# A fourth of the one-hot tiles made by ScalarE, in the preparation stage of a graph-network kernel on Trainium2

## What is computed

```python
w_full = einsum('rb,bdo->rdo', w_comp, weight)      # R=16 types from B=8 bases
x_rel  = einsum('nd,rdo->rno', feat, w_full)        # feat: layer-normed x
msg    = x_rel[etypes, src] * norm
agg    = segment_sum(msg, dst, num_segments=N)
out    = relu(agg + h_bias + feat @ loop_weight)
```

## Time and profile before

| | |
|---|---|
| median of 3 runs | 2738.4 us (2736.8 to 2740.6) |
| profiled execution | 2740.9 us, span 2738.9 us |
| mean granted TensorE clock | 0.919 |
| PE busy | 2204.7 us (80%) |
| POOL busy | 1789.0 us (65%) |
| DVE busy | 952.1 us (35%) |
| ACT busy | 651.5 us (24%) |
| `expand`, first spread to last coefficient copy | about 81.5 to 147.0 us |

### The profile page before, as it was taken

How to read it: one execution, slowest core, us unless ns; L and a number is a source line. 1 busy time by engine, 2 the same in 40 slices (tenths; PEclk the granted TensorE clock), 3 DMA queues, 4 the chain that set the end, 5 groups by cost and what they waited for, 6 DMA issues and landing times. The chain is left out here.

```text
span 2738.9 us, 41332 instructions
## 1 busy us (share of the span) xinstructions
PE 2204.7 (80%) x11549; PEld 1840.7 (67%) x11550; DVE 952.1 (35%) x2094; ACT 651.5 (24%) x1539; POOL 1789.0 (65%) x1888
## 2 busy tenths in 40 slices
PE   2789999999999888887676767557666589999988
PEld 0667787877777666666565555446444479999976
DVE  7734233242243222221321212112112733333339
ACT  3523323233223211211111010000000323222246
POOL 0657777777777777777777777777775045555545
PEclk9999999999999999998898888788777799999999
DMA  7544444444444444444343443333333631222237
GB/s 246 155 138 124 132 116 121 125 124 145 117 124 120 134 120 120 121 121 131 109 121 116 121 116 106 109 105 116 107 105 80 250 138 69 69 70 69 69 110 257
DMA packets 146287, 338.71 MB, mean 124 GB/s; under 512 B 36719, under 2 KB 56335, under 8 KB 145981
## 3 DMA queue, kind: packets, MB, share of 16 engines
q0 software_dynamic: 89328, 245.33, 30.6%
q1 hardware_dynamic: 39351, 59.54, 6.3%
q10 hardware_dynamic: 17526, 32.88, 3.7%
HBM read 292.84 MB, written 47.97 MB: 124 GB/s over the span
## 5 line engine op out<-in xcount | busy, mean ns | idle before, releaser
L1063 POOL DMA_INDIRECT rows<-feat,srcT x1540 | 1460.7, 948 | 491.2 <-issue 439.6
L1266 PE MATMUL psW<-rows,S 128*128 x3920 | 1049.4, 429 | 357.4 <-SPq L1034 325.4
L1266 PEld LDWEIGHTS psW<-rows,S 128*128 128x128 f32 x3920 | 830.7, 216 | 572.1 <-issue 439.5
L1137 DVE TENSOR_TENSOR S<-psHere,coefS 128x896 f32<-128x896 f32 x280 | 301.9, 1090 | 1307.4 <-PE psW L1266 1294.9
L1326 ACT COPY z<-psW 128x512 f32<-128x512 f32 x196 | 114.7, 585 | 1389.3 <-PE psW L1266 1388.7
L1232 PE MATMUL psG<-wb,zT 128*128 128x256 f32 (+1 forms) x1600 | 356.0, 381 | 0.0
L1232 PEld LDWEIGHTS psG<-wb,zT 128*128 128x128 f32 (+1 forms) x1600 | 298.6, 188 | 45.2 <-ACT zT L1337 0.2
L1716 PE MATMUL psH<-xT,w1x 128*128 128x128 f32 x1840 | 227.2, 277 | 2.7 <-issue 2.7
L1667 POOL DMA_INDIRECT expert_rows<-os,at_rows x114 | 116.8, 1024 | 170.7 <-DVE os L1775 170.7
L1716 PEld LDWEIGHTS psH<-xT,w1x 128*128 128x128 f32 x1840 | 216.9, 194 | 4.4 <-issue 4.4
L1725 PE MATMUL psO<-w2s,hT 128*128 x912 | 215.7, 379 | 0.0
(11 more groups left out here) (279 smaller groups left out, 1405.0 us busy)
## 6 DMA issues: line engine op xcount, KB each, us to landing
rows<-feat,srcT POOLq DMA_INDIRECT x1568, 2.7
g<-expert_rows SPq DMA_DIRECT2D x24, 512.0 KB, 5.6
w1s<-in_L_ffn_w SPq DMA_DIRECT2D x8, 1024.0 KB, 9.8
w2s<-in_L_ffn_w SPq DMA_DIRECT2D x16, 512.0 KB, 9.9
feat<-rows SPq DMA_DIRECT2D x24, 256.0 KB, 3.0
fts<-feat ACTq DMA_DIRECT2D x24, 256.0 KB, 2.9
h<-in_x ACTq DMA_DIRECT2D x24, 256.0 KB
y_rows<-y ACTq DMA_DIRECT2D x24, 256.0 KB
```

Source lines behind the costliest of these rows:

```text
L1063: e.indirect_dma_start(rows[:, j % RB * H:(j % RB + 1) * H], None, d.feat, bass.IndirectOffsetOnAxis(ap=srcT[:, j:j + 1], axis=0)).then_in ...
L1137: e.tensor_tensor(S[h0 + h][:, :].rearrange("p (s b n) -> p s b n", s=U, b=B), both[:, h * U:(h + 1) * U, :].unsqueeze(2).to_broadcast([P, ...
L1266: last = e.matmul(psW[:, bass.ds(bank[u], H)], S[h][:, u * ZC:(u + 1) * ZC], rows[:, bass.ds(slot[u], H)], start=False, stop=True, skip_gr ...
```

## The change

Tiles with n % 4 == 3 (15 of the 62) are no longer made by VectorE. ScalarE makes them with two dependent activations: Square of `psE - rel_no` into a new bf16 buffer `away`, then Relu of 1 minus `away` into `hot[n % 2]`. For whole numbers this is 1 where the type is equal and 0 elsewhere. In ScalarE's order `one_hot(n + 1)` stands ahead of the copy of tile n. TensorE's waits go by a helper, `hot_made`, which looks at the semaphore of the engine that makes that tile. VectorE makes two more small constants ahead of the split weights, and two of its pieces of table move from after tiles 11 and 15 to after tiles 12 and 16.

```diff
--- before.py
+++ after.py
@@ -681,6 +681,8 @@
         typ_b = [sb(f"typ_b{i}", [P, P], BF16) for i in range(2)]
         rel = [sb(f"rel{i}", [P, P]) for i in range(2)]
         hot = [sb(f"hot{i}", [P, SUB], BF16) for i in range(2)]
+        away = sb("away", [P, SUB], BF16)
+        no_neg, one_e = sb("no_neg", [P, 1]), sb("one_e", [P, 1])
         part_i = sb("part_i", [P, 1], I32)
         rel_no = sb("rel_no", [P, 1])
         win_no = sb("win_no", [P, WPAD])
@@ -714,6 +716,17 @@
         GN = CS * B
         total = SC // CS
         blk = ctx.enter_context(nc.Block())
+
+        s_far, s_hot_a = sem("far"), sem("hot_by_scalar")
+
+        def by_scalar(n):
+            return n % 4 == 3
+
+        def hot_made(e, n):
+            if by_scalar(n):
+                e.wait_ge(s_hot_a, n // 4 + 1)
+            else:
+                e.wait_ge(s_hot, n + 1 - (n + 1) // 4)
 
         def coefs_at(n):
             return coefS[:, n * GN:(n + 1) * GN] if n < NEAR else late[n % DL][:, :]
@@ -793,6 +806,14 @@
                 e.copy(dstS[:, g * P:g * P + n], psT[g % 2][:, 0:n])
                 e.copy(wgtS[:, g * P:g * P + n], psT[g % 2][:, P:P + n]).then_inc(s_tc, 1)
 
+            def one_hot(n):
+                e.wait_ge(s_pe, n + 1)
+                if n >= 2:
+                    e.wait_ge(s_pc, n - 1)
+                e.activation(away[:, :], psE[n % 2][:, 0:SUB], ACT.Square, bias=no_neg[:, 0:1]).then_inc(s_far, 1)
+                e.wait_ge(s_far, n // 4 + 1)
+                e.activation(hot[n % 2][:, :], away[:, :], ACT.Relu, bias=one_e[:, 0:1], scale=-1.0).then_inc(s_hot_a, 1)
+
             def coefs(n):
                 e.wait_ge(s_pc, n + 1)
                 if n >= NEAR + DL:
@@ -800,12 +821,15 @@
                 e.copy(coefs_at(n), psC[n % 2][:, 0:GN]).then_inc(s_co, 1)
 
             types(0)
+            e.wait_ge(s_wc3, 1)
             for n in range(total):
                 g, q = divmod(n, NQ)
                 if q == 0:
                     group(g)
                 if q == 1 and g + 1 < SG:
                     types(g + 1)
+                if n + 1 < total and by_scalar(n + 1):
+                    one_hot(n + 1)
                 coefs(n)
                 if OP0 <= n < OP0 + EB:
                     i = n - OP0
@@ -830,7 +854,7 @@
                 if q == 0:
                     e.wait_ge(s_tb, g + 1)
                 if n >= 2:
-                    e.wait_ge(s_hot, n - 1)
+                    hot_made(e, n - 2)
                 for a in range(4):
                     k = 4 * q + a
                     last = e.matmul(psE[n % 2][:, a * P:(a + 1) * P], spread[:, k * P:(k + 1) * P], typ_b[g % 2][:, :], start=True, stop=True)
@@ -844,7 +868,7 @@
                     if (n + 1) % NQ == 0:
                         group((n + 1) // NQ)
                     spread_ids(n + 1)
-                e.wait_ge(s_hot, n + 1)
+                hot_made(e, n)
                 if n >= 2:
                     e.wait_ge(s_co, n - 1)
                 for a in range(4):
@@ -862,6 +886,8 @@
             e.wait_ge(s_const, 3)
             ch(e.tensor_single_scalar(part_i[:, :], part_i[:, :], R - 1, ALU.bitwise_and))
             ch(e.tensor_copy(rel_no[:, :], part_i[:, :]))
+            ch.add(e.memset(one_e[:, :], 1.0))
+            ch(e.tensor_scalar(no_neg[:, :], rel_no[:, :], -1.0, None, ALU.mult))
             ch(e.tensor_copy(wc3[0][:, :], wcd[:, :]))
             ch(e.tensor_tensor(rest[:, :], wcd[:, :], wc3[0][:, :], ALU.subtract))
             ch(e.tensor_copy(wc3[1][:, :], rest[:, :]))
@@ -923,6 +949,8 @@
             for n in range(total):
                 if n % NQ == 0 and n // NQ + 1 < SG:
                     local(n // NQ + 1)
+                if by_scalar(n):
+                    continue
                 e.wait_ge(s_pe, n + 1)
                 if n >= 2:
                     e.wait_ge(s_pc, n - 1)
@@ -931,11 +959,11 @@
                     windows_of_steps()
                 if n == 9:
                     banks()
-                if n == 11:
+                if n == 12:
                     clears()
                 if n == 13:
                     places_in_ring()
-                if n == 15:
+                if n == 16:
                     tiles_of_turns()
                 if n == 17:
                     tile_ends()
```

## The result

The changed kernel takes **2742.1 us**, the median of 19 runs (2740.1 to 2743.4), beside 2737.5 us for the kernel before in 19 runs of the same set (2734.0 to 2743.1). The profiled execution after took 2742.12 us with a span of 2740.1.

The account below looks back on a forecast made before the run. `expand` delays the unbroken gather train, so its change passes on whole: 0.7 + 0.0 + 0.5 + 2.3 + 1.1 + 0.5 + 0.75 = +5.9 us on the 2738.4 us median, 2744.3 us; range 2739.4 to 2750.4.

Parts of the forecast that it names:

- three waits per one-hot: ScalarE's queue in `expand`: each `one_hot` adds three waits, 0 to 0.1 us a tile, taken as 0.05, +0.75 us.
- What bounds the kernel: GpSimd's gather train, about 1900 of 2738.9 us, starts after `expand`; within that, a TensorE-VectorE loop through even tiles, 3.44 us.
- The odd chain: Odd tiles in `expand`: with ScalarE's two operations at 1.49 us, this dependent sequence sets rounds of 3.98 us per four tiles.
- ScalarE as the bound with `opened`: From tile 12, where ScalarE also makes `opened`: its own work sets 5.15 us per four tiles; tiles 15 to 27 +2.3.
- Tiles 35 to 59: End of `expand`: six rounds of 3.98 us, with 2.0 of 4.7 us excess left, +0.5 us (bounds -1.5 to +3.2).
- The store rival: Tiles 35 to 59: stores set the pace anyway, that stretch gains 1.5 us; total +3.9, 2742.3 us; chance 0.18.
- The step that failed: From `expand` to the graph layer: any lengthening or shortening of `expand` is passed on whole, as nothing later can start earlier.
- VectorE as the bound: Rounds in `expand`: VectorE's work, 3.1 us of 3.44, sets the pace; -10.6 us, 2727.8 us, faster; chance 0.05.
- ring waits before each one-hot: Tiles 35 to 59: each wait for a store delays a one-hot, 4.7 us stay whole; +8.6, 2747.0 us; chance 0.09.
- table loads: ScalarE's Square one-hots among the Sign activations: two loads each, 8 x 1.28 = +10 us more, 2754.5 us; chance 0.03.
- half clock: Tiles with `opened`: TensorE drops to 1.2 GHz, its own steps double, +3.3, 2747.6 us; chance 0.05.

Follow-up runs that it names:

- the second execution: The changed kernel, unedited, timed and traced once more; ratio 1.0017 (1.0008 to 1.0026).
- the run with one operation: The changed kernel with ScalarE's one-hot cut to its Square, the Relu left out, so coefficients are not the reference's; ratio 0.9992 (0.9982 to 1.0001).
- the run with a pause: The kernel before, with three 128 x 2048 copies on ScalarE ahead of its last coefficient copy in `expand`; ratio 1.0018 (1.0009 to 1.0027).
- The run on even tiles: The changed kernel with ScalarE's 15 one-hots moved to tiles with n % 4 == 2, one table step moved by a tile; ratio 1.0030 (1.0018 to 1.0042).
- the ring of eight: Eight `late` buffers in place of four: in the kernel before, ratio 0.9986 (0.9977 to 0.9995); in the changed kernel, 1.0003 (0.9994 to 1.0012).
- The padded kernel: The changed kernel with 28 one-element memsets added on VectorE at the end of `expand`; ratio 1.0022 (1.0012 to 1.0032).

## Why the prediction was right, point by point

The prediction was 2744.3 us, with 2739.4 to 2750.4 as its range; 2742.1 lies in it, and the sign is right. The forecast lay at the edge of 0.2% and gave 0.53 to a slowdown beyond it and 0.42 to one within; it came out within. By how much each term held (starts of coefficient matmuls, the two first profiles):

| stretch | predicted | measured |
|---|---|---|
| tiles 0 to 3 | +0.7 | +0.56 |
| 3 to 11 | 0.0 | +0.09 |
| 11 to 15 | +0.5 | +0.75 |
| 15 to 27 | +2.3 | +2.15 |
| 27 to 35 | +1.1 | +0.97 |
| 35 to 59 | +0.5 | +1.17; about -1.0 in the second execution; the kernel before alone varies by 2 |
| three waits per one-hot | +0.75 | nothing beyond the above |
| `experts` | not considered | -3.5 |
| behind the last `psH` matmul | not considered | -1.0 |

- *What bounds the kernel* held. That VectorE's share of `expand` was no evidence of a bound was shown by the run with one operation (round 3.44, VectorE's idle time nearly doubled), and that lost time is passed on by the run with a pause.
- *The odd chain* held. ScalarE's two operations start 0.72 us apart and `hot` is there 1.44 after the first one started; forecast 1.49. Round 3.92 for 3.98. The estimate worked out beside it from the Trainium skill (ScalarE: Activation LUTs, What ACT_TABLE_LOAD costs) was 1.44 for the pair, and the trace agrees to the hundredth; the means of 688 and 721 ns lie on both sides of its 0.71.
- *ScalarE as the bound with `opened`* held on odd tiles: 5.05 a round for 5.15, with ScalarE busy for 13.81 of 14 us. The run on even tiles shows that it isn't the whole story (5.57).
- *Tiles 35 to 59*: taking all of the 4.7 us of excess as the stores' was right (the ring of eight removes 4.7). That 2.0 would be left was a guess between bounds; 3.0 and 0.9 were left in two executions. Ring waits fell from 10.5 to 2.9 and 2.8 us. When one was left it held up the one-hot behind it, as foreseen. The store rival gave 2742.3 us, next to the number measured, but that is luck: its stretch (-1.5) was seen only in part and in one execution, and its sum lacks the give-back.
- *The three waits* were priced at 0.05 us a tile and cost nothing that can be seen.
- *The step that failed*: "every microsecond by which `expand` becomes longer or shorter as one that is passed on whole", taken as the only effect on the rest of the kernel. The pass-on is right; that nothing else changes is wrong. The edit also shortens VectorE's program, and `experts` gets 3.5 us shorter in the first profiles (432.9 to 429.4), 2.6 us on the average over all (431.8 to 432.9 against 429.3 to 430.3). The padded kernel, where this is absent, stands at +6.0 us by its ratio (+3.3 to +8.8), beside +5.9 forecast; the changed kernel stands at +3.8 and +4.7. So the forecast was 1 to 2 us too high for the kernel, and its size for `expand` fits what was measured. Single executions give no closer account: against the mean of two of before (149.47), `expand` ended 5.4 and 2.4 us later in two of the changed kernel and 5.4 in the padded one, and with 2.6 given back that would leave less than the whole kernel shows.
- *Rivals.* VectorE as the bound, ring waits before each one-hot and table loads are out. The prediction read one load in the trace; there are two, in the kernel before (L344 and, for the Sqrt in `combine`, L1871) and in the changed one (L344 and L1899), so the Square brought none. The list of fillers in the section that the prediction names for this (the Trainium skill, ScalarE: Activation LUTs, Table sets: the hidden batching unit) has relu, copy, identity and abs; that Square is one of them was the prediction's own reading, and the trace bears it out. TensorE did fall to half clock from about 137.4 to 140.4 us (granted clock 0.53 there), behind the pause of 2.12 us, but that is at tile 47 and not among the tiles with `opened`, and before had such a stretch too.

What stays open: the two microseconds by which the last third of `expand` varies; why the gather train is 1943 us in one execution and 1948 in another (in the three profiles with 1947.4 to 1948.1 a gather takes 951 or 952 ns on the average, in the others 948 to 950, but why isn't shown); the 5.57 us of the even variant; and why VectorE resumes sooner in `experts`.

## What to carry to other kernels

Between two engines with two buffers, the latency around the loop can set the pace and not the busy time, as it did here outside the `opened` stretch: work taken from an engine that is off that loop gives idle time, and work with a longer latency put on it, or on a chain beside it with 0.25 us of slack, gives a slowdown. Look first for depth (here a third buffer and a longer store ring, 0.24%, where the ring alone gave 0.14%), then for balance, and check in whose queue the moved operation stands behind what. And compare the stages that the edit didn't touch: here 16 to 28 instructions fewer on an engine ahead of a later loop moved the time of that loop by 2.6 us, more than half of what the edit cost in all.

## What the runs showed of the hardware

- Length of program on VectorE: 28 or 16 instructions fewer ahead of a later loop took the waits at the starts of its turns from 31.8 to 28.4 us, two turns from 45.4 to 45.1 and the loop from about 432 to 429.7 us; 28 trivial ones put back gave 31.8 and 431.8.
- VectorE's compare of 512 values from PSUM: 0.75 us for one alone, 1.41 for two, 2.72 for four in a row, so about 0.66 apart in a row; I had used 0.71, and from that 3.1 us for a round in which VectorE never waits, which takes 2.82.
- ScalarE: an activation over 512 values from PSUM in f32 took 0.688 us, one from SBUF in bf16 0.721.
- Stores beside the gathers: with four buffers they cost the kernel before 10.5 us of waits and 4.7 us of the stage, with eight none; the kernel gained 0.14%.
